# The recurrence of a decoder block: its output products and two blocks' gating on GpSimd, and its side work in a new order

## The chip, the cores and the metric

The kernel runs on one core of a Trainium2 chip. The core has a matmul engine (PE), a vector engine (DVE), an activation engine (ACT), GpSimd (POOL) and a queue for transfers (SP). The metric is the device time of one execution in microseconds (us), lower is better.

## The reference, cut to what matters

A decoder layer over x (2 sequences of 1024 tokens, 256 wide), in three parts, each followed by a residual sum and a layer norm: a gated linear recurrence, an attention over 64 context rows picked by an index list, and a feed-forward part with its own attention and 8 experts. The change lies in the first part and in the preparation of the second.

```
def _L0_attn_ref(x, Wq, Wk, Wv, Wgk1, Wgk2, bgk2, Wg, gnw, Wo):   # 16 heads, DK = 8, DV = 16
    q, k, v = x @ Wq, x @ Wk, x @ Wv
    gk = jax.nn.log_sigmoid(x @ Wgk1 @ Wgk2 + bgk2) / 16.0
    def step(h, inp):
        qt, kt, vt, gt = inp
        h = h * jnp.exp(gt)[..., None] + kt[..., None] * vt[..., None, :]
        ot = jnp.einsum('bhk,bhkv->bhv', qt * scale, h)
        return (h, ot)
    ...
    o = o * jax.lax.rsqrt(jnp.mean(o * o, axis=-1, keepdims=True) + EPS) * gnw
    o = o * (g * jax.nn.sigmoid(g))                               # g = x @ Wg
    return o.reshape(Bx, Tx, VDIM) @ Wo
...
x = _layernorm(x + _L0_attn_ref(...))
x = _layernorm(x + _L0_xattn_ref(x, ctx, indices, ...))   # softmax over 64 picked context rows
x = _layernorm(x + _L0_ffn_ref(x, ...))
```

For the second part the kernel doesn't gather: it counts, per token, how often each of the 64 context rows is in the index list, and adds the logarithm of the count to the scores.

## The kernel before

The program is a few blocks of work with a barrier of all engines between them. The first, `front`, holds the recurrence; `cross_blocks` follows, then the attention and the experts. In each, every engine has its own list of instructions, written out by hand in the order in which it runs them; semaphores tie the lists together. An engine that waits holds up all that is behind it in its list.

The recurrence keeps (head, key index) on the 128 partitions and the 1024 tokens of one sequence along the row. One **step** jj (32 of them, `NJ`: 16 value indices for each of two sequences) does:

- PE, `values(jj)`: four matmuls that spread one value index over the partitions, into PSUM banks 0 and 1 or 2 and 3 (`2 * (jj % 2)`), two steps ahead of their use.
- DVE, `product(jj)` (L521): values times keys, from PSUM into a slot of the ring `qh` (6 slots, `RQ`).
- DVE, `state(jj)` (L526): the scan over the tokens with `decay`, in place in `qh`.
- DVE, `output(jj)` (L531): `qh` times the queries `QT`, in place.
- Each fourth step, with q the number of the four: PE `sums(q)` (L314) adds the 8 key indices of a head for those four steps; ACT `sums_out(q)` copies the sums out, PE `turn(q)` transposes them, ACT `tokens(q)` writes them into `O`, token by token. Banks 4 and 5 carry this, and all the other projections in turn.

DVE's list is `state(jj)`, side work of the step, `product(jj + 1)`, `output(jj)`, more side work. Side work is written as `if jj == ...` in each engine's list: the second sequence's projections and gates, the low parts of values (`parts_lo`) and of x (`x_lo`), output gates (`output_gates` on PE, `silu` on ACT), weights of the second part (`wqo`, `udc`, `ckv`, `kv`), and the counting. For this ACT makes 65 **indicators** (`signs`, L696, tile `c_hot`: the sign of index minus a constant, ring of 6 slots, `RS`), and PE's `counts(u)` sums four at a time into banks 6 and 7. The table `taken` says how many indicators ACT has made by each step, and `count_at` derives from it the step of each `counts(u)`.

When a sequence's outputs are whole, its two blocks of 512 tokens go on: ACT squares (`out_square`), DVE sums per head (`out_means`), ACT takes the root (`out_root`), DVE `out_gated` (a reciprocal L846, `O` times it L848, times the gates L850), PE transposes, ACT copies, PE multiplies with `Wo` and adds x (`out_product`), DVE takes the statistics from PSUM (`out_stats`), ACT writes the normed rows (`out_rows`). Blocks 0 and 1 are done inside the recurrence (steps 17 to 28), 2 and 3 in `cross_blocks`. At step 30 DVE spreads the second part's keys and values (`Kblk`, L602, and `Vblk`). After step 31 come the last indicator, the counts' way out (`cntT`), and the first pieces of the second part; then the barrier.

## Time and profile before

| | us |
|---|---|
| median of 3 runs | 1363.28 (1363.03 to 1363.65) |
| the profiled execution, its own time | 1363.14 |
| its span in the profile | 1361.4 |
| recurrence, from the first scan to the end of the last indicator | 24.58 to 193.98 |
| next block's first matmul | 208.86 |

The profiled execution is within 0.2 us of the median, and 1.7 us of it lie outside the span; all places below are us from the span's start. Busy shares say which engine could be the limit; what ends last at a place is read from the order in time and from the idle time in brackets.

### The profile page before, as it was taken

Reading aid. Unit: us, or ns where it says so; the run is one execution under the profiler, and the core shown is the slowest. Engines: PE = TensorE matmul, PEld = TensorE weight load, DVE = VectorE, ACT = ScalarE, POOL = GpSimd, SP = SyncE. Lnnn points to the kernel's source line nnn. Section 1 sums busy time; section 2 is a strip of 40 time slices with the busy share of each in tenths; the row PEclk is TensorE's granted clock in tenths of the full one; section 3 lists DMA queues with packets and bytes.
Section 4 is the critical chain, followed back from the end, with each engine's and each line's share of the span. In section 5 each row is a group of like instructions: output and inputs, shape, how many; then the busy total and the mean of one; then the engine's idle time right before and its main releaser. Section 6 shows DMA issues by size and latency. Waiting matters only on the chain.

```text
span 1361.4 us, 19541 instructions
## 1 busy us (share of the span) xinstructions
PE 1283.8 (94%) x7802; PEld 953.8 (70%) x7802; DVE 973.9 (72%) x1481; ACT 642.8 (47%) x942; POOL 140.5 (10%) x225
## 2 busy tenths in 40 slices
PE   8787768999899999999999999999999999999997
PEld 6354436677655555558888788888888888888886
DVE  7899997787798998848676655655646556555566
ACT  5687764346468877874332432323323223233233
POOL 5000003000523423310000000000000000000000
PEclk9898889999999999999999999999999999999999
DMA  5000001004602221203000011201101102010001
GB/s 140 1 1 1 0 1 36 2 1 147 209 27 67 64 56 51 68 20 109 17 1 17 16 58 43 70 16 39 47 8 47 39 17 70 16 39 16 0 16 47
DMA packets 40332, 55.82 MB, mean 41 GB/s; under 512 B 9553, under 2 KB 26625, under 8 KB 40241
## 3 DMA queue, kind: packets, MB, share of 16 engines
q1 hardware_dynamic: 35056, 43.67, 10.5%
q0 software_dynamic: 3648, 10.09, 2.6%
q8 instruction: 62, 1.02, 0.3%
q10 hardware_dynamic: 1536, 0.81, 0.2%
q14 instruction: 30, 0.24, 0.1%
HBM read 43.73 MB, written 10.55 MB: 40 GB/s over the span
## 4 chain that ended last, share of the span: by engine, by line
PE 52%; DVE 2%; ACT 0%; issue 0%; ACTq 0%; DVEq 0%
PE PS L2513 25%; PE PS L2526 24%; PE PS L2276 1%; PE PS L114 0%; PE PS L2539 0%; PE PS L2257 0%; PE PS L2290 0%; DVE OT_all L2674 0%; DVE r_st L2352 0%; DVE r_on L2369 0%; DVE r_on L2349 0%; PE PS L2551 0%; DVE X L2361 0%; DVE x_mid L2665 0%; ACT X L2635 0%
## 5 line engine op out<-in xcount | busy, mean ns | idle before, releaser
L2596 ACT ACTIVATE x_g<-PS,x_bias 128x512 f32<-128x512 f32 x256 | 175.9, 687 | 493.4 <-PE PS L2513 493.3
L2513 PE MATMUL PS<-x_h,x_w 128*128 128x512 f32 x1536 | 398.7, 395 | 0.0
L2526 PE MATMUL PS<-x_mid,x_w 128*128 128x512 f32 x1488 | 383.9, 393 | 1.1 <-DVE x_w L2248 1.1
L2513 PEld LDWEIGHTS PS<-x_h,x_w 128*128 128x128 f32 x1536 | 286.1, 188 | 64.7
L2526 PEld LDWEIGHTS PS<-x_mid,x_w 128*128 128x128 f32 x1488 | 279.2, 188 | 65.7 <-DVE x_w L2248 1.6
L2665 DVE CAST x_mid<-x_g 128x512 fp32r<-128x512 f32 x256 | 109.2, 427 | 267.3 <-ACT x_g L2596 266.9
L2115 DVE TENSOR_REDUCE a_M<-PS 128x2 f32<-128x1024 f32 (+1 forms) x144 | 173.1, 1223 | 24.5 <-PE PS L1812 18.2
L2667 DVE TENSOR_TENSOR x_mid<-x_g,x_mid 128x512 fp32r<-128x512 f32 x256 | 177.3, 693 | 8.8
L2053 ACT ACTIVATE f_parts<-PS 128x512 f32<-128x512 f32 x224 | 120.8, 601 | 36.2 <-PE PS L1866 24.8
L1889 PE MATMUL PS<-f_parts,aV 128*32 128x256 f32 (+1 forms) x960 | 75.1, 394 | 0.2 <-POOL f_parts L1700 0.2
L696 ACT ACTIVATE c_hot<-c_idxT,c_cid 128x1024 bf16<-128x1024 bf16 x65 | 70.6, 1138 | 5.2 <-PE PS L337 3.9
L526 DVE TENSOR_TENSOR_SCAN qh<-decay,qh 128x1024 f32<-128x1024 f32 x32 | 73.0, 2281 | 0.0
L2493 POOL DMA_DIRECT2D x_wb<-route_w x31 | 16.9, 545 | 476.1 <-DVE OT_all L2674 450.1
L1866 PE MATMUL PS<-aQ,aK 64*128 64x512 f32 x192 | 50.8, 485 | 0.5 <-ACT f_h L2053 0.5
L1866 PEld LDWEIGHTS PS<-aQ,aK 64*128 64x128 f32 x192 | 20.3, 183 | 37.1 <-ACT f_parts L2053 27.0
L2674 DVE SCALAR_TENSOR_TENSOR OT_all<-PS,x_bias,x_wb 128x512 f32<-128x512 f32 x62 | 46.2, 745 | 0.0
L1700 POOL TENSOR_SCALAR_AFFINE_SELECT f_parts<-f_parts 128x512 f32<-128x512 f32 x45 | 28.7, 637 | 161.9 <-ACT f_parts L2053 142.4
L307 PE MATMUL PS<-vparts,g_sel 128*128 128x512 f32 x128 | 39.5, 433 | 5.5 <-DVE qh L521 4.9
L1808 PE MATMUL PS<-aK,aQ 64*128 64x512 f32 (+3 forms) x256 | 36.2, 327 | 7.2 <-PEq L1061 2.8
L2248 DVE TENSOR_TENSOR x_w<-x_raw,x_w 128x1024 fp32r<-128x1024 f32 x32 | 39.4, 1233 | 1.4 <-ACT x_w L2243 1.4
L521 DVE TENSOR_TENSOR qh<-PS,KT 128x1024 f32<-128x1024 f32 x32 | 38.6, 1205 | 1.2 <-PE PS L314 1.2
L531 DVE TENSOR_TENSOR qh<-qh,QT 128x1024 f32<-128x1024 f32 x32 | 38.9, 1214 | 0.0
(385 smaller groups left out, 1577.9 us busy)
## 6 DMA issues: line engine op xcount, KB each, us to landing
x_raw<-L_ffn_e_w SPq DMA_DIRECT2D x32, 512.0 KB, 3.8
qk_parts<-f_parts SPq DMA_DIRECT2D x16, 512.0 KB, 3.5
x_wb<-route_w POOLq DMA_DIRECT2D x31, 256.0 KB, 3.4
aQ<-qk_parts SPq DMA_DIRECT2D x96, 64.0 KB, 2.5
aK<-qk_parts SPq DMA_DIRECT2D x60, 64.0 KB, 2.7
X<-x SPq DMA_DIRECT2D x4, 512.0 KB, 7.5
aK<-qk_parts SPq DMA_DIRECT2D x36, 48.0 KB, 2.0
out<-X SPq DMA_DIRECT2D x3, 512.0 KB, 3.5
```

The costliest lines, as they stand in the source:

```text
L526: e.tensor_tensor_scan(qh[:, jj % RQ, :], decay[:, batch(jj // HD)], qh[:, jj % RQ, :], 0.0, ALU.mult, ALU.add).then_inc(s_h, 1)
L696: e.activation(hot[:, n % RS, :], self.idxT[:, :], ACT.Sign, bias=self.cid[:, c:c + 1], scale=2.0).then_inc(s_sg, 1)
L1866: last = e.matmul(bank, K[q][R, s, tile(TB * h if kind == "k0" else kind)], Q[q][R, s, q0:q0 + BLK], start=True, stop=True)
L1889: last = e.matmul(PS[32 * j:32 * j + 32, 7, dst:dst + w], Vs[m % 2][:, kt, j, :], x, start=k in (0, 3) and half == 0, stop=k in (2, NQD - ...
L2053: e.activation(buf[k][:, j, :], PS[:, 4 + b % 3, :], ACT.Exp).then_inc(A.sem, 1)
L2115: e.tensor_reduce(dst, src, AX.X, ALU.max, negate=True).then_inc(VC.sem, 1)
L2513: last = e.matmul(PS[:, f % 2, :], w1[n % 2][u][:, kt, f * P:(f + 1) * P], self.rows(v, k)[:, kt, :], start=m == 0 and kt == 0, stop=m == ...
L2526: last = e.matmul(PS[:, 2 + 2 * (it % 2) + d, :], w2[n % 2][v][:, f, d * P:(d + 1) * P], mid[u][:, f % RM, :], start=f == 0 and m == 0, st ...
L2596: e.activation(g[s % RG][:, :], PS[:, f % 2, :], ACT.Gelu, bias=b1[:, n, f:f + 1]).then_inc(A.sem, 1)
L2665: e.tensor_copy(mid[0][:, f % RM, :], g[s % RG][:, :]).then_inc(V.sem, 1)
L2667: e.tensor_tensor(mid[1][:, f % RM, :], g[s % RG][:, :], mid[0][:, f % RM, :].bitcast(F32), ALU.subtract).then_inc(V.sem, 1)
L2674: e.scalar_tensor_tensor(out=(y if n else sumT[k])[:, d, :], in0=PS[:, 2 + 2 * (it % 2) + d, :], scalar=b2[:, n, d:d + 1], in1=wb[:, it % ...
```

## The change

It does the following.

1. `output(jj)` for steps 0 to 30 goes from DVE to GpSimd's list; output 31 stays on DVE. `product(jj)` writes back into the PSUM banks that it read, and `state(jj)` scans from there into `qh`. `values(jj)` now waits for `state(jj - 2)` (s_h) where it waited for `product(jj - 2)` (s_kv). `qh` has 7 slots.
2. Of 65 indicators, 17 go to GpSimd (`indicator`, a comparison), 48 stay on ACT. `counts(u)` waits for both. A comparison gives 0 or 1 where the sign gives -1 or 1, so new constants (`fix`, `winb`) correct the counts.
3. For blocks 0 and 1 GpSimd does the two products of the gating (`out_gated_pool`), and the normed rows (`out_rows_pool`); DVE keeps the reciprocal (L905 of the changed kernel). ACT stores the unnormed rows in X (`out_stored`), and DVE's statistics read them there. `Kblk` is spread by GpSimd too.
4. `sums_out`, `turn` and `tokens` work in halves of 512 tokens. The side work of PE, ACT and DVE stands at other steps.

The diff, cut to its core (of the new order of side work only some lines, of `taken` the new table's line):

```diff
-        RQ, RS = 6, 6
+        RQ, RS = 7, 6
...
-            self.og[m] = z[:, :].rearrange("p (t d) -> p t d", t=TB)
+            self.og[m] = (KT[:, 0:T] if m else z[:, :]).rearrange("p (t d) -> p t d", t=TB)
...
+        of_scalar = [n for n in range(NCTX) if n % 4 < 3]
+        taken = list(itertools.accumulate((2, 2, 1, 0, 0, 2, 2, 1, 0, 0, 1, 2, 2, 1, 3, 1, 2, 1, 2, 1, 0, 1, 2, 2, 3, 1, 2, 3, 2, 1, 3, 2)))
+        count_at = [next((jj for jj in range(5, NJ) if taken[jj - 1] >= 3 * u + 3), NJ) for u in range(16)]
+        def output(e, jj):
+            e.wait_ge(s_h, jj + 1)
+            if jj % HD == 0:
+                e.wait_ge(A.sem, A.at(f"q{jj // HD}"))
+            e.tensor_tensor(qh[:, jj % RQ, :], qh[:, jj % RQ, :], QT[:, batch(jj // HD)], ALU.mult).then_inc(s_qh, 1)
...
+                def indicator(u):
+                    if u:
+                        e.wait_ge(s_cnt, min(u, 15))
+                    n = 4 * u + 3 if u < 16 else NCTX
+                    e.tensor_scalar(hot[:, n % RS, :], self.idxT[:, :], float(3 * 16 + u), None, ALU.is_ge).then_inc(s_hot, 1)
+                def keys(b, g):
+                    e.tensor_tensor(Kblk[:, b, g, :, :], kT[...], self.m16[...], ALU.mult).then_inc(s_kblk, 1)
+                e.wait_ge(A.sem, A.at("idx"))
+                indicator(0)
+                for jj in range(NJ - 1):
+                    output(e, jj)
+                    for u in range(1, 16):
+                        if jj == (5, 6, 8, 12, 14, 16, 18, 20, 23, 24, 26, 27, 28, 29, 30)[u - 1]:
+                            indicator(u)
+                    if jj in (21, 25):
+                        self.out_gated_pool(e, (jj - 21) // 4, s_gate)
+                    if jj in (22, 23, 24, 25):
+                        if jj == 22:
+                            e.wait_ge(A.sem, A.at("kv"))
+                        keys((jj - 22) // KD, (jj - 22) % KD)
+                    elif jj == 28:
+                        self.out_rows_pool(e, 0, s_row)
+                indicator(16)
+                self.out_rows_pool(e, 1, s_row)
...
                     if jj >= 2:
-                        e.wait_ge(s_kv, jj - 1)
+                        e.wait_ge(s_h, jj - 1)
...
-                    e.wait_ge(s_sg, min(4 * u + 4, NCTX + 1))
+                    if u < 16:
+                        e.wait_ge(s_sg, 3 * u + 3)
+                    e.wait_ge(s_hot, u + 1)
...
-                e.wait_ge(s_kv, NJ)
+                e.wait_ge(s_row, 1)
+                e.wait_ge(s_h, NJ - 1)
                 self.c_turn(e, 0)
...
-                    e.tensor_tensor(qh[:, jj % RQ, :], wide(2 * (jj % 2)), KT[:, batch(jj // HD)], ALU.mult).then_inc(s_kv, 1)
+                    e.tensor_tensor(wide(2 * (jj % 2)), wide(2 * (jj % 2)), KT[:, batch(jj // HD)], ALU.mult).then_inc(s_kv, 1)
...
+                    if jj >= RQ:
+                        e.wait_ge(s_s, 2 * ((jj - RQ) // 4) + 2)
+                    e.tensor_tensor_scan(qh[:, jj % RQ, :], decay[:, batch(jj // HD)], wide(2 * (jj % 2)), 0.0, ALU.mult, ALU.add).then_inc(s_h, 1)
...
                 for jj in range(NJ):
                     state(jj)
+                    if jj + 1 < NJ:
+                        product(jj + 1)
+                    else:
+                        output(e, jj)
...
+                    elif jj == 21:
+                        self.out_reciprocal(e, 0)
...
+                    elif jj == 25:
+                        self.out_reciprocal(e, 1)
+                    elif jj == 26:
+                        self.out_stats_stored(e, 0)
...
-                e.activation(self.cntT[:, :], wide(6), ACT.Copy).then_inc(s_fin, 1)
+                e.activation(self.cntT[:, :], wide(6), ACT.Identity, bias=self.fix[:, 0:1], scale=self.fix[:, 1:2]).then_inc(s_fin, 1)
...
+    def out_gated_pool(self, e, m, done):
+        og = self.og[m]
+        e.wait_ge(self.OV[m].sem, self.OV[m].at("rs"))
+        e.tensor_tensor(self.by_head(og), self.by_head(self.out_tiles(self.O, m)), self.o_rs[m][:, :].unsqueeze(2).broadcast_to((P, TB * H, HD)), ALU.mult).then_inc(done, 1)
+        e.wait_ge(done, 2 * m + 1)
+        e.tensor_tensor(og, og, self.out_tiles(self.G, m), ALU.mult).then_inc(done, 1)
...
+    def out_rows_pool(self, e, m, done):
+        e.wait_ge(self.OV[m].sem, self.OV[m].at("nmr"))
+        for t in range(TB):
+            x = self.X[:, m * TB + t, :]
+            last = e.tensor_scalar(x, x, self.o_rstd[m % 2][:, t:t + 1], self.o_nmr[m % 2][:, t:t + 1], ALU.mult, ALU.add)
+        last.then_inc(done, 1)
```

Three places show the order. **DVE, step 19, before** (L526 is the scan, L514 `parts_lo`, L521 the product, L531 the output, L846 to L850 the reciprocal and the gating):

```order
L526 SCALAR_TENSOR_TENSOR qh<-decay,qh 128x1024
L514 TENSOR_TENSOR vparts<-PS,vparts 128x1024
L521 TENSOR_TENSOR qh<-PS,KT 128x1024
L531 TENSOR_TENSOR qh<-qh,QT 128x1024
L846 RECIPROCAL go_rs<-go_rs 128x64
L848 TENSOR_TENSOR z<-O,go_rs 128x1024
L850 TENSOR_TENSOR z<-z,G 128x1024
```

**DVE, step 19, changed** (L574 scan, L567 product, L888 `out_means`, L562 `parts_lo`):

```order
L574 SCALAR_TENSOR_TENSOR qh<-decay,PS 128x1024
L567 TENSOR_TENSOR PS<-PS,KT 128x1024
L888 TENSOR_REDUCE go_ms<-z 128x64
L562 TENSOR_TENSOR vparts<-PS,vparts 128x1024
L574 SCALAR_TENSOR_TENSOR qh<-decay,PS 128x1024
```

Outputs and gating have left the list; between two scans there is one product and the side work, and the scan now follows the product whose result it reads at once.

**GpSimd, end of the first block, before** (L225 and L1062 are the way to the next block):

```order
L943 AFFINE_SELECT c_selaug<-c_selaug 128x256 [waits cs_pool] x4
L250 DMA Wo<-L_attn_Wo 128x2x256
L252 DMA gnw<-L_attn_gnw 16x1 x8
L225 UNCONDITIONAL_BRANCH
L1062 UNCONDITIONAL_BRANCH [waits barrier_Pool_Activation_PE_DVE_SP_gather]
L1064 MEMSET aug 128x4x48
L1065 MEMSET c_halfc 128x128
```

**GpSimd, steps 21 to 24, changed** (L231 output, L910 and L912 gating, L267 keys, L265 indicator; in brackets the semaphores waited for):

```order
L231 TENSOR_TENSOR qh<-qh,QT 128x1024 [waits gs_h]
L910 TENSOR_TENSOR z<-O,go_rs 128x1024 [waits go_dve0]
L912 TENSOR_TENSOR z<-z,G 128x1024 [waits gs_gate]
L231 TENSOR_TENSOR qh<-qh,QT 128x1024 [waits gs_h]
L267 TENSOR_TENSOR c_Kblk<-c_L,c_m 128x512 [waits g_act]
L231 TENSOR_TENSOR qh<-qh,QT 128x1024 [waits gs_h]
L265 TENSOR_SCALAR c_hot<-c_idxT 128x1024 [waits gs_cnt]
L267 TENSOR_TENSOR c_Kblk<-c_L,c_m 128x512
L231 TENSOR_TENSOR qh<-qh,QT 128x1024 [waits gs_h]
L265 TENSOR_SCALAR c_hot<-c_idxT 128x1024 [waits gs_cnt]
L267 TENSOR_TENSOR c_Kblk<-c_L,c_m 128x512
```

A list that was empty there now carries the outputs, the gating behind output 21, the keys and the indicators.

**PE, steps 17 and 18, before** (L307 values, L431 and L434 transposes `udc`, L292 turned values):

```order
L307 MATMUL PS<-vparts,g_sel 128x512 [waits gs_lo,gs_kv]
L307 MATMUL PS<-vparts,g_sel 128x512 x3
L431 MATMUL PS<-ident,c_up 128x128 [waits gs_tok]
L431 MATMUL PS<-ident,c_up 128x128 x3
L434 MATMUL PS<-ident,c_down 128x128 x2
L434 MATMUL PS<-ident,c_ctx 128x128 x2
L307 MATMUL PS<-vparts,g_sel 128x512 [waits gs_lo,gs_kv]
L307 MATMUL PS<-vparts,g_sel 128x512 x3
L292 MATMUL PS<-XTp,Wvp 128x512 [waits g_act]
L292 MATMUL PS<-XTp,Wvp 128x512 x11
```

**PE, steps 20 and 21, changed** (L340 values, L477 and L480 `udc`, L484 `ckv`, L347 `sums`, L354 `turn`):

```order
L340 MATMUL PS<-vparts,g_sel 128x512 [waits gs_lo,gs_h]
L340 MATMUL PS<-vparts,g_sel 128x512 x3
L477 MATMUL PS<-ident,c_up 128x128 [waits g_act]
L477 MATMUL PS<-ident,c_up 128x128 x3
L480 MATMUL PS<-ident,c_down 128x128 x2
L480 MATMUL PS<-ident,c_ctx 128x128 x2
L484 MATMUL PS<-decay 128x128 [waits g_act]
L484 MATMUL PS<-decay 128x128
L340 MATMUL PS<-vparts,g_sel 128x512 [waits gs_lo,gs_h]
L340 MATMUL PS<-vparts,g_sel 128x512 x3
L347 MATMUL PS<-qh,headsum 32x512 [waits gs_qh,g_act]
L347 MATMUL PS<-qh,headsum 32x512 x7
```

The `udc` and `ckv` steps now stand together in step 20, each behind a copy on ACT, ahead of the next values; before, other values and projections stood between them.

## Rows read from the trace of the kernel before

**Rows 1.** Busy time by stretch: span, each engine's busy us (instructions), PE clock, DMA

```profile
24.58:194.00 169.42, 127.03 (x717) 77.92 (x715) 161.62 (x134) 120.38 (x127) 0.00 (x0) 0.89 0.00 1
...
608.00:1361.40 753.40, 741.24 (x3385) 607.08 (x3385) 457.04 (x816) 239.18 (x332) 19.00 (x35) 1.00 0.11 34
```

**Rows 2.** DVE in order of time: first scan, a plain step, gating, last output. Start us, us, instruction

```profile
24.58 2.29 DVE L526 TENSOR_TENSOR_SCAN qh<-decay,qh 128x1024 f32<-128x1024 f32 x1
...
93.50 2.28 DVE L526 TENSOR_TENSOR_SCAN qh<-decay,qh 128x1024 f32<-128x1024 f32 x1
95.70 1.20 DVE L521 TENSOR_TENSOR qh<-PS,KT 128x1024 f32<-128x1024 f32 x1
96.82 1.22 DVE L531 TENSOR_TENSOR qh<-qh,QT 128x1024 f32<-128x1024 f32 x1
97.95 2.28 DVE L526 TENSOR_TENSOR_SCAN qh<-decay,qh 128x1024 f32<-128x1024 f32 x1
...
128.13 0.55 DVE L846 RECIPROCAL go_rs<-go_rs 128x64 f32<-128x64 f32 x1
128.71 1.23 DVE L848 TENSOR_TENSOR z<-O,go_rs 128x1024 f32<-128x1024 f32 x1
129.97 1.23 DVE L850 TENSOR_TENSOR z<-z,G 128x1024 f32<-128x1024 f32 x1
...
195.05 1.23 DVE L531 TENSOR_TENSOR qh<-qh,QT 128x1024 f32<-128x1024 f32 x1
```

**Rows 3.** DVE groups to 270 us: count, busy us, mean ns, idle before

```profile
L526 DVE TENSOR_TENSOR_SCAN qh<-decay,qh 128x1024 f32<-128x1024 f32 x32 | 73.0, 2281 | 0.0
L531 DVE TENSOR_TENSOR qh<-qh,QT 128x1024 f32<-128x1024 f32 x32 | 38.9, 1214 | 0.0
L521 DVE TENSOR_TENSOR qh<-PS,KT 128x1024 f32<-128x1024 f32 x32 | 38.6, 1205 | 1.2 <-PE PS L314 1.2
```

**Rows 4.** GpSimd groups, whole span

```profile
L1700 POOL TENSOR_SCALAR_AFFINE_SELECT f_parts<-f_parts 128x512 f32<-128x512 f32 x45 | 28.7, 637 | 161.9 <-ACT f_parts L2053 142.4 <-ACT f_parts L2073 18.5
...
L1677 POOL TENSOR_TENSOR aV<-V,f_bv 128x512 f32<-128x512 f32 x8 | 10.3, 1284 | 0.8 <-POOLq L1707 0.2
```

**Rows 5.** DVE and GpSimd at work together: at 12 us, and at 352 us

```profile
12.10 1.16 DVE L502 TENSOR_TENSOR Wkp<-c_Kblk,Wkp 128x256 fp32r<-128x256 f32 x1 [0.19 <-ACT Wqp L713]
13.18 0.41 DVE L502 TENSOR_TENSOR Wqp<-c_Kblk,Wqp 128x256 fp32r<-128x256 f32 x1
...
11.82 1.17 POOL L943 TENSOR_SCALAR_AFFINE_SELECT c_selaug<-c_selaug 128x1024 fp32r<-128x1024 f32 x1
...
353.70 1.40 DVE L1516 SCALAR_TENSOR_TENSOR f_parts<-PS,f_bk,f_parts 128x512 fp32r<-128x512 f32 x2
...
352.69 1.30 POOL L1677 TENSOR_TENSOR aV<-V,f_bv 128x512 f32<-128x512 f32 x1
```

**Rows 6.** PE in order of time in the recurrence: start us, us, instruction, idle before

```profile
47.10 3.64 PE L314 MATMUL PS<-qh,headsum 128*32 128x512 f32 x16 [3.25 <-DVE XTp L505]
...
101.34 1.19 PE L307 MATMUL PS<-vparts,g_sel 128*128 128x512 f32 x4
102.36 3.03 PE L283 MATMUL PS<-Wgp,XTp 128*128 128x256 f32 x24
...
109.55 1.93 PE L314 MATMUL PS<-qh,headsum 128*32 128x512 f32 x16 [0.27 <-ACT c_WoutT L768]
...
118.35 0.60 PE L431 MATMUL PS<-ident,c_up 128*128 128x128 f32 x4
```

**Rows 7.** ACT in order of time: `udc` copy, root's table load, `ckv` copy, last indicators

```profile
119.42 0.60 ACT L776 ACTIVATE decay<-PS 128x512 f32<-128x512 f32 x1 [1.12 <-PE PS L434]
...
124.71 1.28 ACT L841 ACT_TABLE_LOAD   x1
...
187.39 0.38 ACT L794 ACTIVATE c_L<-PS 128x256 f32<-128x256 f32 x1
187.65 6.33 ACT L696 ACTIVATE c_hot<-c_idxT,c_cid 128x1024 bf16<-128x1024 bf16 x6
```

389 lines of the change are left out of this document (207 added, 182 removed).

## The prediction, made before the changed kernel ran

> **What bounds the kernel now.** I read the busy time by stretch first. From 608 us on PE works 741.24 of 753.40 us, so nothing but PE's own work counts there, and the change doesn't touch it. The stretch from 24.58 to 194 is the recurrence, 169.42 us, and there DVE works 161.62, PE 127.03, ACT 120.38 and GpSimd nothing [rows 1]. Then I read DVE's instructions in order of time. A plain step starts at 93.50 and the next at 97.95: 4.45 us, as scan to product 2.20, product to output 1.12, output to scan 1.13, with no gap [rows 2]. 32 such steps are 142 us; the rest is side work. The groups say the same: 73.0, 38.6 and 38.9 us, no idle time to speak of before them [rows 3]. DVE's list sets the pace. The last ACT indicators end at 187.65 + 6.33 = 193.98 [rows 7], and the next block's first matmul comes at 208.86, 14.9 us later. In the changed kernel the same chain follows the last indicator: counts, their copy, transposes, DVE's pieces. So the question is where the last indicator ends, and the time moves by as much.
>
> **DVE's list up to step 21.** The output, 1.13 us of each step, leaves. The scan now stands right behind the product that it needs. A pair that depends on each other so is the gating: it starts at 128.71 and at 129.97, 1.26 apart, where independent ones start 1.12 apart [rows 2]. So a step is 2.20 + 1.26 = 3.46 us. That the product writes PSUM and the scan reads it has no row. The nearest: a product that reads PSUM takes 1205 ns, one from the SBUF 1214 [rows 3]. I take no difference; from -0.01 to +0.06 us for each of 64 instructions the bounds are -1 and +4 us. State 21 ends after 21 steps and a scan, 21 x 3.46 + 2.28 = 74.9, plus seven pieces of side work of some 1.13 each (`parts_lo` three times, `x_lo` twice, `log_sigmoid`, `out_means`), 7.9: 82.8 us.
>
> **What PE adds there.** `values(jj + 2)` now waits for `state(jj)`, and its product is due when `state(jj + 1)` ends: from 8 us the room shrinks to under 3.5. PE's list has other pieces between two `values` (1.0 from its start to the next piece's, 101.34 to 102.36 [rows 6]). With two steps' 6.9 us, two `values` and about 1 us of hops, a piece of up to 3.8 us hides. Most do: `output_gates` is 3.0, a sum 1.9 at full rate [rows 6]. Where pieces stand close they don't: steps 13 to 16 have sums with a turn that waits for ACT's copies, then two `output_gates` with a table load between them. By adding them up I find DVE held 1.0 and 1.9 us there, 0.2 at step 9 and 1.2 at step 19, where `parts_lo(3)` waits for ACT's copy of the turned values. Together 4.3 us. PE at half rate is dearer: the sums after an idle time of 3.25 us took 3.64 us, others 1.93 [rows 6]. The clock over the stretch is 0.89 [rows 1]; with shorter gaps I take one such spell on the path, 1.7 us.
>
> **DVE and GpSimd in each other's way.** At 12.10 a DVE subtraction with both inputs in the SBUF took 1.16 us; the next, of the same form, took 0.41. GpSimd's select ran from 11.82 to 12.99: DVE stood until it ended. At 353.70 two DVE instructions with one SBUF input and one from PSUM took 1.40 together, beside a GpSimd product of 1.30 us; that is what others of GpSimd's products take, 1284 ns [rows 4, 5]. So one kind waits and the other doesn't. New products and scans are of the second kind: the scan's other input is in PSUM. Only `log_sigmoid(1)` (z and decay) is of the first; it meets an output in flight, half of 2.46 us, 1.2 us. The Trainium skill's page "SBUF — State Buffer", section "Who interferes with whom", puts it as a rule, two SBUF inputs against a GpSimd instruction that reads the SBUF; the trace agrees, and by it these 1.2 us stand and no others.
>
> State 21 ends at 24.58 + 82.8 + 4.3 + 1.7 + 1.2 = 114.6.
>
> **GpSimd's list.** Its product of 128x512 takes 1284 ns; a select takes 637 for 512 columns and 1.17 us for 1024, so some 107 ns are fixed [rows 4, 5]. An output of 1024 columns is then 2 x 1284 - 107 = 2.46 us (between 2.3 and 2.57). It hides under DVE's 3.46, with the indicators of 1.17 (the select's time; the comparison has no row, 0.9 to 1.5). From step 21 it doesn't: the gating of block 0 starts when DVE's reciprocal is there. Behind that stand nine outputs (22.1), four gating products (9.8), four keys of 1.28 (5.1), eight indicators (9.4) and one block's rows, four of 0.37 (1.5): 47.9 us, where DVE has ten steps and some 7 us of side work, 42. GpSimd sets the end. A block's gating products take DVE 2.4 us now [rows 2] and will take GpSimd 4.9.
>
> **The reciprocal comes late.** PE's step 20 is a chain, counted from the end of state 20: `values` 1.1, `udc` transposes 1.2 (the row at 118.35 is half of it), ACT's two copies 1.1, `ckv` 0.7, its copies 0.7, the root's table load 1.28 and root 0.35, reciprocal 0.55, six hops 0.6 [rows 2, 6, 7]: 7.6 us, 4.1 past the end of state 21. DVE stands in front of the reciprocal for 2.2 of them; GpSimd starts the gating then.
>
> **Waits at the end.** PE's `counts(u)` wait for GpSimd's indicators, PE's product of block 1 for the gating, ACT's copy for PE, and ACT's last six indicators (1.05 each [rows 7]) for all of these. Followed through, `counts(14)` is done 2.7 us after GpSimd could start indicator 15, and ACT's last indicator ends within 0.5 us of GpSimd's. Last indicator: 114.6 + 4.1 + 47.9 + 2.7 = 169.3. Before it was 193.98: 24.7 us less. ACT's saving, 17 indicators of 1.05, is 18 us off the path. The profiled execution, 1363.14, lies 0.14 under the median, 1363.28, and I subtract from the median: 1338.6 us.
>
> **Rivals.** (1) *GpSimd and PE keep up.* Outputs of 2.3 us, indicators near 1.0, no wait of 4.1 or 2.7: 13 products at 0.16 less are 2.1, eight indicators at 0.17 less 1.4, and the waits go but for 2: 8.3 us more, 33 less than now, 1330. For it, the waits are sums of small hops that may overlap; against, lists in order rarely lose nothing. DVE's own list with no wait (82.8, ten steps 34.6, side work 7.0, last output 1.2: 125.6) would end 46 us earlier than now, when the last output ends at 195.05 + 1.23 [rows 2]: 1317, a floor. (2) *PE's order binds.* PE's 127 us at clock 0.89 in 145 us are 88%. If each of the seven turns in the loop holds PE 1.2 us for ACT's copies on the path (8.4), and the 4.3 double: 12.7 back, 12 us less, 1351. (3) *DVE and GpSimd take turns*, the side that ends slower: place, every step; if a scan or product stands for the whole output, a step is 3.46 + 2.46 = 5.9 us where it was 4.45, 31 x 1.45 = 45 us more, 1408. It decides from 1.0 us of each output not covered. For it: the 1.16 us at 12.10; against: the pair at 353.70 [rows 5]. The Trainium skill's "Perfetto Trace Analysis", section "Optimizing Scalar/DVE Operations", warns that moving work between these two may not help, since they share a read port: this rival. (4) The saving is eaten altogether, within 0.2%: needs (2) twice.
>
> **The numbers.** Forecast 0.57, (1) 0.13, (2) 0.20, (3) 0.08, (4) 0.02. A measurement of this kernel can tell about 0.2% from no change, 2.7 us. Faster 0.90, same 0.02, slower 0.08. The range holds (1) and (2) and PSUM's bound: 1325 to 1354.
>
> **What would show it.** DVE steps of 3.46 us and no product over 1.25 or scan over 2.35; `log_sigmoid` longer than 1.22; GpSimd outputs near 2.46, back to back only after step 21; DVE idle before the reciprocal for ACT; the last indicator near 169 us, the time from there to the next block unchanged, near 14. Scans of 3 us or outputs of 4 would show (3); `values` late in most steps, (2). If the next block starts later than the last indicator says, my reading of the tail is wrong.

## The result, and the profile after

| | before | after |
|---|---|---|
| median, us | 1363.47 (4 runs, 1363.03 to 1365.45) | 1351.9 (4 runs, 1350.68 to 1353.2) |
| ratio, 95% interval | | 0.9915, 0.9899 to 0.9931 |
| profiled span, us | 1361.4 | 1349.5 |
| state 21 ends | | 119.76 (forecast 114.6) |
| last indicator ends | 193.98 | 181.80 (forecast 169.3) |
| next block's first matmul | 208.86 | 197.20 |

The change is worth 11.6 us; the forecast was 24.7 (1338.6 us). The time lies in the stated range, 1325 to 1354, but more than half of the forecast gain is missing.

Busy time by stretch of the changed kernel (columns as in [rows 1]):

```profile
24.58:182.00 157.42, 121.97 (x719) 79.44 (x718) 127.34 (x97) 103.58 (x119) 134.46 (x61) 0.92 0.00 1
596.00:1349.50 753.50, 741.26 (x3385) 607.09 (x3385) 456.77 (x816) 239.14 (x332) 18.87 (x35) 1.00 0.11 34
```

The recurrence takes 157.42 us instead of 169.42. DVE's busy share fell from 95% [rows 1] to 81%, and GpSimd works 134.46 us, 85%. After it nothing has changed: from 596 us on PE works 741.26 us, against 741.24 in [rows 1].

DVE in order of time (start us, us, instruction, idle before it and who ended that): a plain step, the waits at 61, 67 and 103 us and the long subtraction ahead of state 21, state 21, the reciprocal, and a wait behind it.

```profile
28.39 2.29 DVE L574 TENSOR_TENSOR_SCAN qh<-decay,PS 128x1024 f32<-128x1024 f32 x1
30.59 1.21 DVE L567 TENSOR_TENSOR PS<-PS,KT 128x1024 f32<-128x1024 f32 x1
31.84 2.29 DVE L574 TENSOR_TENSOR_SCAN qh<-decay,PS 128x1024 f32<-128x1024 f32 x1
...
61.37 1.23 DVE L567 TENSOR_TENSOR PS<-PS,KT 128x1024 f32<-128x1024 f32 x1 [2.52 <-PE PS L340]
...
67.07 1.23 DVE L567 TENSOR_TENSOR PS<-PS,KT 128x1024 f32<-128x1024 f32 x1 [2.15 <-PE PS L340]
...
71.65 2.53 DVE L559 SCALAR_TENSOR_TENSOR z<-z,decay 128x1024 f32<-128x1024 f32 x1
...
103.49 1.23 DVE L567 TENSOR_TENSOR PS<-PS,KT 128x1024 f32<-128x1024 f32 x1 [4.30 <-PE PS L340]
...
117.47 2.29 DVE L574 TENSOR_TENSOR_SCAN qh<-decay,PS 128x1024 f32<-128x1024 f32 x1
...
122.61 0.55 DVE L905 RECIPROCAL go_rs<-go_rs 128x64 f32<-128x64 f32 x1 [1.73 <-ACT go_rs L892]
...
162.38 1.23 DVE L567 TENSOR_TENSOR PS<-PS,KT 128x1024 f32<-128x1024 f32 x1 [3.01 <-PE PS L340]
```

DVE's groups, and GpSimd's (count, busy us, mean ns of one, idle before):

```profile
L574 DVE TENSOR_TENSOR_SCAN qh<-decay,PS 128x1024 f32<-128x1024 f32 x32 | 72.9, 2278 | 1.4 <-PE PS L347 0.8
L567 DVE TENSOR_TENSOR PS<-PS,KT 128x1024 f32<-128x1024 f32 x32 | 38.9, 1214 | 13.8 <-PE PS L340 13.8
...
L231 POOL TENSOR_TENSOR qh<-qh,QT 128x1024 f32<-128x1024 f32 x31 | 73.5, 2376 | 17.2 <-DVE qh L574 17.2
L265 POOL TENSOR_SCALAR c_hot<-c_idxT 128x1024 bf16<-128x1024 bf16 x17 | 47.1, 2769 | 7.0 <-ACT c_idxT L765 4.2 <-PE PS L374 2.5
L953 POOL TENSOR_SCALAR X<-X,go_rstd,go_nmr 128x256 f32<-128x256 f32 x8 | 4.3, 554 | 0.0
L267 POOL TENSOR_TENSOR c_Kblk<-c_L,c_m 128x512 f32<-128x512 f32 x4 | 4.2, 1052 | 0.0
```

The step is what it was to be: 31.84 - 28.39 = 3.45, a scan 2278 ns, a product 1214, although one writes and the other reads PSUM. GpSimd's output takes 2376 ns. Its indicator takes 2769, where 1.17 us had been put.

GpSimd in order of time from state 21 on, then PE (three places ahead of state 21, and the end of the stage) and ACT:

```profile
121.59 2.36 POOL L231 TENSOR_TENSOR qh<-qh,QT 128x1024 f32<-128x1024 f32 x1
123.91 1.93 POOL L910 TENSOR_TENSOR z<-O,go_rs 128x1024 f32<-128x1024 f32 x1
...
176.22 5.60 POOL L265 TENSOR_SCALAR c_hot<-c_idxT 128x1024 bf16<-128x1024 bf16 x2
181.80 2.17 POOL L953 TENSOR_SCALAR X<-X,go_rstd,go_nmr 128x256 f32<-128x256 f32 x4
...
57.96 1.98 PE L306 MATMUL PS<-c_L,Wgk 16*128 16x512 f32 x4 [2.16 <-ACT c_L L784]
...
62.23 3.86 PE L296 MATMUL PS<-XTp,Wkp 128*128 128x512 f32 x12
...
97.90 4.63 PE L316 MATMUL PS<-Wgp,XTp 128*128 128x256 f32 x24 [1.75 <-ACT V L712]
...
179.12 1.05 PE L371 MATMUL PS<-c_hot,c_win 128*32 128x512 bf16 x8 [3.85 <-POOL c_hot L265]
181.87 1.04 PE L374 MATMUL PS<-c_hot,c_win 128*32 128x512 bf16 x2 [1.71 <-POOL c_hot L265]
...
197.20 0.98 PE L1196 MATMUL PS<-XTp,vparts 64*128 64x256 f32 x12 [1.31 <-PEq L233]
...
175.30 2.17 ACT L738 ACTIVATE c_hot<-c_idxT,c_cid 128x1024 bf16<-128x1024 bf16 x2
```

From 123.91 to 181.80 GpSimd runs without a gap: 57.9 us for the list that was put at 47.9. ACT is done with its indicators at 177.47; PE waits 3.85 and 1.71 us for GpSimd's last two, and the next block follows as before, 15.4 us behind the last indicator (14.9 before).

### The profile page after: what moved, and what is told of

Read it like the earlier page. It is cut to its first block, busy times and chain, and to the rows that moved or that the text cites. A ratio compares the mean times of both kernels' runs of the same rounds, so it can differ in the third digit from the quotient of the medians.

```text
span 1349.5 us, 19595 instructions
## 1 busy us (share of the span) xinstructions
PE 1280.6 (95%) x7802; PEld 957.5 (71%) x7802; DVE 936.8 (69%) x1442; ACT 626.0 (46%) x936; POOL 277.6 (21%) x297
## 4 chain that ended last, share of the span: by engine, by line
PE 52%; DVE 2%; ACT 0%; issue 0%; ACTq 0%; DVEq 0%
PE PS L2602 25%; PE PS L2615 25%; PE PS L2365 1%; PE PS L114 0%; PE PS L2628 0%; PE PS L2346 0%; PE PS L2379 0%; DVE OT_all L2763 0%; DVE r_st L2441 0%; DVE r_on L2458 0%; DVE r_on L2438 0%; PE PS L2640 0%; DVE X L2450 0%; DVE x_mid L2754 0%; ACT X L2724 0%
## 5 line engine op out<-in xcount | busy, mean ns | idle before, releaser
L2204 DVE TENSOR_REDUCE a_M<-PS 128x2 f32<-128x1024 f32 (+1 forms) x144 | 173.1, 1223 | 24.2 <-PE PS L1901 18.0
L231 POOL TENSOR_TENSOR qh<-qh,QT 128x1024 f32<-128x1024 f32 x31 | 73.5, 2376 | 17.2 <-DVE qh L574 17.2
L574 DVE TENSOR_TENSOR_SCAN qh<-decay,PS 128x1024 f32<-128x1024 f32 x32 | 72.9, 2278 | 1.4 <-PE PS L347 0.8
L738 ACT ACTIVATE c_hot<-c_idxT,c_cid 128x1024 bf16<-128x1024 bf16 x48 | 52.5, 1136 | 11.4 <-PE PS L371 10.1
L265 POOL TENSOR_SCALAR c_hot<-c_idxT 128x1024 bf16<-128x1024 bf16 x17 | 47.1, 2769 | 7.0 <-ACT c_idxT L765 4.2
L567 DVE TENSOR_TENSOR PS<-PS,KT 128x1024 f32<-128x1024 f32 x32 | 38.9, 1214 | 13.8 <-PE PS L340 13.8
L1955 PEld LDWEIGHTS PS<-aQ,aK 64*128 64x128 f32 x192 | 20.4, 183 | 37.0 <-ACT f_parts L2142 26.0
L340 PE MATMUL PS<-vparts,g_sel 128*128 128x512 f32 x128 | 37.3, 415 | 6.7 <-DVE qh L574 5.8
```

The lines of the kernel that those rows point to most:

```text
L231: e.tensor_tensor(qh[:, jj % RQ, :], qh[:, jj % RQ, :], QT[:, batch(jj // HD)], ALU.mult).then_inc(s_qh, 1)
L574: e.tensor_tensor_scan(qh[:, jj % RQ, :], decay[:, batch(jj // HD)], wide(2 * (jj % 2)), 0.0, ALU.mult, ALU.add).then_inc(s_h, 1)
L738: e.activation(hot[:, n % RS, :], self.idxT[:, :], ACT.Sign, bias=self.cid[:, c:c + 1], scale=2.0).then_inc(s_sg, 1)
L1955: last = e.matmul(bank, K[q][R, s, tile(TB * h if kind == "k0" else kind)], Q[q][R, s, q0:q0 + BLK], start=True, stop=True)
L2204: e.tensor_reduce(dst, src, AX.X, ALU.max, negate=True).then_inc(VC.sem, 1)
```

## The experiments

Each kernel was compared with the kernel before on the same chip; the changed kernel was measured twice, and beside it ran only e6, e7 and e8 (with its second measurement). From one such comparison to the next the median before lay between 1360.6 and 1363.5 us, so the ratios are compared; the column in us is the ratio times 1361 (1363.5 for the first row), less that. "Stage" is the start of the next block's first matmul in the profiled run, "rest" the span from there to the end. Stage and rest come from one profiled execution of each kernel, so small differences in them mean little: e14 and e16 have the same lists up to state 21, and it ended at 122.1 and 120.1 us. The named runs:

| run | edit to the changed kernel | ratio (95%) | us to before | stage | rest |
|---|---|---|---|---|---|
| before | | 1 | 0 | 208.86 | 1152.5 |
| the change | none, first measurement | 0.9915 (0.9899-0.9931) | -11.6 | 197.20 | 1152.3 |
| e5_change | none, second measurement | 0.9937 (0.9919-0.9954) | -8.6 | 197.42 | 1152.2 |
| e2_late_dve | late 8 indicators on DVE | 0.9888 (0.9873-0.9902) | -15.2 | 188.75 | 1155.4 |
| e3_early_dve | early 9 indicators on DVE | 0.9954 (0.9939-0.9968) | -6.3 | 200.11 | 1153.4 |
| e4_gate_dve | gating on DVE | 0.9937 (0.992-0.9954) | -8.6 | 201.01 | 1153.9 |
| e6_gates_later | one gate product later on PE | 0.9929 (0.9909-0.9949) | -9.7 | 193.68 | 1153.3 |
| e7_both | e2 and e6 | 0.9864 (0.9847-0.988) | -18.5 | 186.48 | 1153.1 |
| e8_twice_late | 2 late indicators twice | 0.9979 (0.9967-0.999) | -2.9 | 204.17 | 1155.2 |
| e9_twice_early | 2 early indicators twice | 0.993 (0.9912-0.9948) | -9.5 | 199.03 | 1153.1 |
| e10_fill | fills for the 17 indicators | 0.985 (0.9834-0.9865) | -20.4 | 185.60 | 1153.0 |
| e12_fill_gates | e10 and e6 | 0.9837 (0.982-0.9854) | -22.2 | 183.53 | 1155.7 |
| e13_two_ops | indicator with a second operation | 1.0004 (0.9992-1.0017) | +0.5 | 206.29 | 1154.9 |
| e14_two_ops_gates | e13 and e6 | 1.0007 (0.9995-1.0019) | +1.0 | 208.47 | 1153.7 |
| e16_and_signs | e14, two ACT indicators earlier | 1.0005 (0.9994-1.0015) | +0.7 | 206.40 | 1153.2 |
| e17_dve_signs | e7, two ACT indicators earlier | 0.9875 (0.9858-0.9892) | -17.0 | 187.93 | 1154.0 |
| e18_split | e17, two indicators back on GpSimd | 0.9852 (0.9837-0.9866) | -20.1 | 187.41 | 1152.2 |

The theory after the result: GpSimd's list sets the end from state 21 on, and the indicator in it costs 1.6 us more than had been put. The rival: PE's order and ACT's chains hold the stage in any case.

### What the indicator costs (e1_ops, e11_ops2, e15_ops3)

> The cost by itself: as soon as the indices stand in their tile, GpSimd runs two fills and eight more instructions on 128x1024 elements, each after the one before has ended: the comparison with bf16 in and out, with f32 in and out, f32 in and bf16 out, bf16 in and f32 out; the product with one number in bf16 and in f32; the bf16 comparison on half the columns; a copy in f32. Nothing is left out of the rest. The comparison that the change gives to GpSimd took 2.77 us a piece where I had put 1.17. If it is the comparison that is slow, the two products take 1.2 to 1.5 and the four comparisons 2.8. If it is the 16-bit type, the f32 comparison takes 1.2 to 1.5 (or 2.2, four times the 0.54 of a row product of 128x256) and the bf16 product 2.8. If it is GpSimd's pace for any arithmetic on one input, all lie at 2.1 to 2.8 and the half at 1.4. The whole kernel becomes later by no more than the sum of these instructions, about 20 us.

Three lists of single instructions on GpSimd, ahead of its first indicator, of this form:

```
+ e.memset(F, 1.0).then_inc(s_m, 1)
+ for out, src, op in ((Bf, Bf, ALU.is_ge), (F, F, ALU.is_ge), (Bf, F, ALU.is_ge), (F, Bf, ALU.is_ge), (Bf, Bf, ALU.mult), ...):
+     e.wait_ge(s_m, 2 + nm)
+     e.tensor_scalar(out, src, 1.0, None, op).then_inc(s_m, 1)
```

The first list on GpSimd, in order of time (`Bf` bf16, `F` f32):

```profile
29.57 2.80 POOL L277 TENSOR_SCALAR c_hot<-c_hot 128x1024 bf16<-128x1024 bf16 x1
32.45 2.77 POOL L277 TENSOR_SCALAR c_Kblk<-c_Kblk 128x1024 f32<-128x1024 f32 x1
...
41.01 2.78 POOL L277 TENSOR_SCALAR c_hot<-c_hot 128x1024 bf16<-128x1024 bf16 x1
...
46.72 1.49 POOL L277 TENSOR_SCALAR c_hot<-c_hot 128x512 bf16<-128x512 bf16 x1
48.28 1.04 POOL L280 COPY c_Kblk<-c_Kblk 128x1024 f32<-128x1024 f32 x1
```

Comparison or product, bf16 or f32, in or out: all 2.77 to 2.80 us. Only the fill (0.96, ahead of these), the copy (1.04) and half of the columns (1.49) are cheaper. So it is neither the comparison nor the type, and of the three cases of the expectation the last holds. But one row of the changed kernel speaks against "GpSimd's pace for one input": a row product of 128x256, with two operations, takes 554 ns [groups above], four of them 2.17 us for 1024 columns.

> The cost by itself, once more: the changed kernel with two fills and eight instructions in f32 on GpSimd ahead of its first indicator, to find why four row products of 128x256 (two operations, factors from a tile) take 2.17 us and one comparison of 128x1024 with a plain number takes 2.77. In turn: multiply and add with factors from a tile on 1024 columns; the same with plain numbers; multiply alone with a factor from a tile; multiply and add from a tile on 256 columns; multiply alone by a plain number on 256; the product of two tiles on 1024; the comparison with a factor from a tile on 1024. If a plain number is what is slow, the forms with factors from a tile take 2.1 to 2.2 for 1024 columns and the others 2.8. If one operation is slower than two, multiply alone takes 2.8 in both forms. If it is the length, 256 columns take under 0.6 in both and 1024 take 2.8 in both.

```profile
29.98 1.20 POOL L280 TENSOR_SCALAR c_Kblk<-c_Kblk,eps 128x1024 f32<-128x1024 f32 x1
31.26 1.05 POOL L282 TENSOR_SCALAR c_Kblk<-c_Kblk 128x1024 f32<-128x1024 f32 x1
32.42 2.85 POOL L284 TENSOR_SCALAR c_Kblk<-c_Kblk,eps 128x1024 f32<-128x1024 f32 x1
35.37 0.56 POOL L280 TENSOR_SCALAR c_Kblk<-c_Kblk,eps 128x256 f32<-128x256 f32 x1
36.01 0.85 POOL L286 TENSOR_SCALAR c_Kblk<-c_Kblk 128x256 f32<-128x256 f32 x1
```

In order: multiply and add with factors from a tile 1.20, with plain numbers 1.05; multiply alone 2.85; multiply and add on 256 columns 0.56, multiply alone 0.85; behind them two tensors 2.37, and the comparison with its factor from a tile 2.84. Two operations are cheaper than one: with the factor from a tile 1.20 against 2.85. That asked for the obvious edit, a comparison with a second operation that does nothing.

> The cost by itself, third list on GpSimd: compare and multiply by a number in bf16 and in f32; multiply and add in bf16; compare and add in f32; multiply twice in f32; add alone in f32; compare and multiply in bf16 on half the columns; a copy in bf16. If only the count of operations decides, all with two take 1.05 to 1.2 us on 1024 columns and the one with one takes 2.8. If multiply and add is a fast case of its own, the other pairs take 2.8 or more. If 16-bit tiles are slower in the two-operation form, the bf16 rows stand out.

```profile
29.69 3.66 POOL L280 TENSOR_SCALAR c_hot<-c_hot 128x1024 bf16<-128x1024 bf16 x1
33.44 3.63 POOL L280 TENSOR_SCALAR c_Kblk<-c_Kblk 128x1024 f32<-128x1024 f32 x1
37.15 1.04 POOL L280 TENSOR_SCALAR c_hot<-c_hot 128x1024 bf16<-128x1024 bf16 x1
38.28 4.77 POOL L280 TENSOR_SCALAR c_Kblk<-c_Kblk 128x1024 f32<-128x1024 f32 x2
```

Compare and multiply takes 3.66 (bf16) and 3.63 (f32), multiply and add in bf16 1.04. The row at 38.28 holds two instructions, compare and add, and multiply twice; in a narrower window the first of them is 3.64 us long, which leaves some 1.1 for the second. Behind them adding alone took 2.78. So on GpSimd two arithmetic operations take 1.05 us (1.20 with factors from a tile), one operation (compare, multiply or add) 2.8, and a comparison with a second operation 3.6. The comparison has no cheap form among those tried. The forecast had its price from a select that took 1.17 us for 1024 columns [rows 5], another instruction.

### Does that price set the time (e13_two_ops, e14_two_ops_gates, e16_and_signs)

> The changed kernel with one word more in GpSimd's indicator: compare, and then multiply by 1.0, in the same instruction; the same result, the same places and waits. The second run of single operations showed 128x1024 with two operations at 1.20 and 1.05 us and with one operation at 2.85. If it is the single operation that is slow, whatever the operation is, the indicator falls from 2.77 to 1.05 to 1.2 us, which is the 1.17 that I had put, and this kernel comes to where the one with fills came: 19 to 22 us under the kernel before. If comparisons are slow in either form (the fast rows so far were multiply and add), it stays at 2.8 us and the kernel within 1 us of the changed one.

```
- e.tensor_scalar(hot[:, n % RS, :], self.idxT[:, :], float(3 * 16 + u), None, ALU.is_ge).then_inc(s_hot, 1)
+ e.tensor_scalar(hot[:, n % RS, :], self.idxT[:, :], float(3 * 16 + u), 1.0, ALU.is_ge, ALU.mult).then_inc(s_hot, 1)
```

GpSimd's group of indicators:

```profile
L265 POOL TENSOR_SCALAR c_hot<-c_idxT 128x1024 bf16<-128x1024 bf16 x17 | 61.7, 3628 | 7.0 <-ACT c_idxT L765 4.2 <-PE PS L374 1.0 <-PE PS L371 0.8
```

The cheap price was expected and the dear one came, 3628 ns: neither of the two cases in the expectation. As a measurement it is as good as a dose: 0.86 us more in each of 17 indicators and nothing else, and the whole gain of the change is gone, 1.0004. The stage ends 9.1 us later. State 21 ends where it did, at 119.96; GpSimd's gating behind it starts 1.0 us later, since the indicator just ahead of output 21 is longer, and the list from there to the last indicator takes 66.2 us instead of 57.9: 8.3 us for eight indicators, of which 6.9 are the dose and the rest small gaps between the instructions. Two kernels stood on top of it:

> Two operations in the indicator and the fourth block's gate product in PE's turn 16. With indicators at 1.05 to 1.2 us: the stage ends 2 us before that of the run with two operations alone (the fills with and without this move: first matmul of the next block at 183.5 and 185.6 us) and the time is 20 to 24 us under the kernel before, about what was forecast for the change. If the stage's gain is given back by half clock in the next blocks, as in the profiled runs with the moved product so far, the time is the same as without it.

```
  elif jj == 14:
      e.wait_ge(s_tok, 6)
      output_gates(2, 4)
- elif jj == 15:
+ elif jj == 16:
      e.wait_ge(A.sem, A.at("G2"))
      output_gates(3, 4)
```

> As the kernel with two operations and the moved gate product, and one step more: ACT takes two of its last six indicators ahead of the seventh sums instead of behind them, where it stood idle for 1.6 and 2.0 us. With GpSimd's list out of the way, the end of the stage was ACT's six indicators in a row behind those sums (6.4 us, PE waiting 3.7 and 2.4 us for them). If this is what ends last, up to 2.2 us less than the kernel without this step; if DVE's or GpSimd's last work is right behind, 0 to 1 us less.

```
- taken = ... 3, 2, 1, 3, 2)))
+ taken = ... 3, 2, 2, 2, 2)))
- early = min((0, 2, ... 1, 1, 1, 0, 1, 0)[jj], taken[jj] - taken[jj - 1])
+ early = min((0, 2, ... 1, 1, 1, 2, 1, 0)[jj], taken[jj] - taken[jj - 1])
```

1.0007 and 1.0005: the 20 us were expected of a price that wasn't there. That doesn't say that PE's order is without effect. Here the moved gate product brought state 21 no nearer (122.1 in e14 and 120.1 in e16, against 119.96 in e13); in e14 PE then stood 1.93 us for GpSimd's longer indicator ahead of the sums. In e6_gates_later below, with the shorter indicator, the same move brought it 3.5 us nearer, and the stage followed. What holds in all of them is the distance from the end of state 21 to the stage's end: 77.2 to 77.6 us in the changed kernel, e5, e6 and e9 with indicators of 2.77 us, and 86.3 to 86.4 in e13, e14 and e16 with indicators of 3.63. ACT's two indicators made earlier in e16 changed nothing in that distance (86.30).

### The price taken away (e10_fill, e12_fill_gates)

> What the change would have given at the price that I put on the indicator: the seventeen comparisons on GpSimd are replaced by a fill of the same tile with zeros (0.96 us a piece by the run that measured the operations; my estimate was 1.17), so the counts of a quarter of the contexts come out wrong; every wait, every other instruction and its place stay. Theory (the price of the indicator is the term that failed): GpSimd's list after state 21 falls from 57.9 to 43 us, waits of PE for it go, DVE's end and ACT's last indicators take over at 171 to 174 us, and the kernel is 15 to 19 us under the one before instead of 8 to 12. What is left to the 24.8 us forecast, 6 to 10 us, is then PE's waits ahead of state 21 and ACT's chain at the end. Rival (the price hardly matters, since PE's order holds DVE): within 2 us of the changed kernel.

```
- e.tensor_scalar(hot[:, n % RS, :], self.idxT[:, :], float(3 * 16 + u), None, ALU.is_ge).then_inc(s_hot, 1)
+ e.memset(hot[:, n % RS, :], 0.0).then_inc(s_hot, 1)
```

The fill leaves the comparison out, and the counts of a quarter of the contexts come out wrong; waits and places are the same. The kernel is 20.4 us under the kernel before, where the change is 8.6 and 11.6 under it. GpSimd at the end of the stage, and PE's wait there:

```profile
167.66 1.84 POOL L265 MEMSET c_hot<- 128x1024 bf16 x2 [3.06 <-PE PS L371]
...
166.54 1.04 PE L371 MATMUL PS<-c_hot,c_win 128*32 128x512 bf16 x8 [3.68 <-ACT c_hot L738]
```

GpSimd now waits, 3.06 us, and PE waits for ACT's indicators, 3.68. The end has passed to ACT's chain, as expected; 15 to 19 us had been expected, 20.4 came. The cost of the indicator alone, 1.81 us less in each, is worth 9 to 12 us. All of it lies behind state 21: with nine cheaper indicators ahead of it, state 21 still ended at 119.88.

> The two causes together: the fills in place of the seventeen comparisons (the counts of a quarter of the contexts come out wrong) and the fourth block's gate product in PE's turn 16 instead of 15. If my two terms, the indicator's price and PE's longest wait ahead of state 21, are what separates the forecast of 24.8 us from the result, this kernel lies 18 to 23 us under the one before, 2.5 to 3.7 us under the run with the fills alone in the stage itself. If it lies at the same time as that run, something after state 21 that neither edit touches (ACT's chain to the last indicators) is the end, and state 21 was not.

The edit is that of e10_fill with that of e14_two_ops_gates. 22.2 us under before, and the stage another 2.1 us earlier (183.53 against 185.60), where 2.5 to 3.7 had been expected; by the ratios 0.9837 and 0.985, whose intervals overlap, the step between them is not resolved. With both edits the kernel comes within 2.5 us of the 24.7 forecast. That is in part luck: a fill takes 0.96 us where the forecast had 1.17 (eight of them, 1.7 us), and most of the wait that was taken away stood in the forecast.

### Doses on GpSimd (e8_twice_late, e9_twice_early)

> A dose of GpSimd time after state 21: the indicators of steps 26 and 28 are computed twice, the second time over the first with the same result, 2 x 2.77 = 5.5 us more on GpSimd's list and nothing on another engine. Theory (GpSimd's list is what sets the end from state 21 on): the whole dose arrives, 5 to 6 us more than the changed kernel beside it. Rival (PE's and ACT's chains set it, and GpSimd's indicators hide beside them): 0 to 2 us more.

```
+ twice, s_twice = (11, 13), self.sem("gs_twice")
...
+ if u in twice:
+     e.tensor_scalar(hot[:, n % RS, :], self.idxT[:, :], float(3 * 16 + u), None, ALU.is_ge).then_inc(s_twice, 1)
+     e.wait_ge(s_twice, twice.index(u) + 1)
```

5.5 us more on GpSimd behind state 21 gave 5.6 us more than the changed kernel on the same chip (1358.34 against 1352.78; the interval of this difference is some 3 us to either side). The dose arrived.

> The same dose of GpSimd time as in the run with two late indicators computed twice (which arrived whole: 5.6 us over the changed kernel), now before state 21: the indicators of steps 6 and 14 are computed twice, 5.5 us more on GpSimd. Theory: GpSimd has gaps there (1.6, 3.4, 1.1 us at 70 to 80, 4.3 us at 107) that take it up, and only what PE waits for that one indicator can reach DVE: 0 to 1.5 us more than the changed kernel. Rival (GpSimd's time counts wherever it is spent): 5 us more.

The same with `twice = (2, 5)`. The same dose ahead of state 21 gave 0.993, against 0.9937: no effect that can be resolved; the stage of the profiled run ends 1.6 us later, and by the intervals up to some 2.5 us can't be excluded, the 5.5 can. GpSimd's time costs little or nothing ahead of state 21 and full price behind it. That is the plainest thing shown here, and it names the list that sets the end.

### Who could take the indicators (e2_late_dve, e3_early_dve)

> The eight indicators after step 21 (of the seventeen) are computed by DVE with the same instruction and the same result; the first nine stay on GpSimd. GpSimd's list from state 21 loses 8 x 2.77 = 22.2 us, DVE gets eight instructions of 0.3 to 1.2 us (its bf16 comparison stands in no trace yet), 3 to 9 us. Theory (GpSimd's list sets the end of this stage): GpSimd's list, 57.9 us from the first gating product on, becomes 36 us and no longer binds; the last indicator (181.8 us now) comes at 174 to 178, when DVE's own list ends with the new work in it, and the time is 1344 to 1348. PE's waits for GpSimd of 3.0, 4.1, 1.7 and 3.9 us go. Rival (PE's order and ACT's chains hold the stage in any case): the last indicator stays at 180 to 183 and the time at 1351 to 1353, with DVE waiting as long as before.

```
+ for u in on_vector:                       # in DVE's list, behind product(jj + 1)
+     if jj == {..., 9: 23, 10: 25, 11: 26, 12: 28, 13: 29, 14: 30, 15: 31, 16: 31}[u]:
+         indicator_on(e, u, s_hotv)        # the same instruction, on DVE
```

15.2 us under before, 0.9888: better than the change; the interval overlaps a little with that of the change's first measurement and lies below that of its second. The last indicator ended at 173.1, 1 us ahead of the expected 174 to 178, and the stage 8.5 us earlier than in the changed kernel; the time, 1345.3, is in the expected range. Its own surprise is the price on DVE:

```profile
130.02 0.48 DVE L221 TENSOR_SCALAR c_hot<-c_idxT 128x1024 bf16<-128x1024 bf16 x1
...
138.83 1.82 DVE L221 TENSOR_SCALAR c_hot<-c_idxT 128x1024 bf16<-128x1024 bf16 x1
...
172.30 0.76 DVE L221 TENSOR_SCALAR c_hot<-c_idxT 128x1024 bf16<-128x1024 bf16 x2
...
138.00 2.36 POOL L238 TENSOR_TENSOR qh<-qh,QT 128x1024 f32<-128x1024 f32 x1
```

The same instruction takes 0.48 us where a GpSimd output was just ending, 0.38 a piece at the end when GpSimd had no work, and 1.82 when a GpSimd output (138.00 to 140.36) was in flight: it ended 0.3 us after that. One engine standing until the other's instruction has ended is what the prediction's rows at 12.10 showed, here called the lock: a bf16 comparison with one SBUF input waits too. The Trainium skill's page "SBUF — State Buffer", section "Who interferes with whom", says that DVE's two-port modes, which `tensor_scalar` can enter, are locked out for a whole GpSimd instruction; the trace agrees, 1.6 to 1.8 us against 0.4.

> The mirror of the run before it: the first nine indicators (before state 21) are computed by DVE, the last eight stay on GpSimd. GpSimd loses 9 x 2.77 = 25 us in a stretch in which it stands idle for some 20 of 88 us, DVE gets nine instructions of 0.3 to 1.2 us in the stretch in which its list is followed back to back. Theory: taking work off GpSimd here is worth nothing, DVE's new work moves state 21 from 119.8 to 123 to 128 (less what it hides in DVE's own waits of 2.5, 2.2 and 4.3 us), and with it the end: 1353 to 1360. Rival (GpSimd's load counts everywhere, through the slots of states and through PE's waits for indicators): faster than 1351.9 by some us.

6.3 us under before, 0.9954: 2.3 us (against the 0.9937 run) or 5.3 us (against 0.9915) worse than the change. Nine indicators of some 1.7 us, 15 us, went into DVE's list; state 21 ended at 123.5, 3.7 us later, since DVE's waits for PE took up most of the rest (1.8 us of them are left of 10.9). That GpSimd lost 25 us ahead of state 21 brought nothing to be seen. The theory held in sign and place, though against the second measurement of the change the intervals overlap; for the price on DVE there had been only bounds.

### The gating part undone (e4_gate_dve)

> The one part 'gating of two blocks on GpSimd' undone: DVE computes the two normalizing and the two gating products right behind its reciprocals (four instructions of 1.2 us, 4.9 us), and GpSimd's list loses 1.93 + 2.36 + 1.95 + 2.35 = 8.6 us. Theory: GpSimd's list ends earlier until it meets DVE's last states, which come 4.9 us later: after state 30 (165.9 us now, some 170.8 then) an output and two indicators of 2.4 + 5.6 us are still due, so the last indicator at 179 (181.8 now) and the time 1349, in any case not over 1352. Rival (DVE's and PE's orders set the end): slower by the 4.9 us that DVE gets, 1356 to 1357.

```
- self.out_gated_pool(e, (jj - 21) // 4, s_gate)      # GpSimd, steps 21 and 25
- self.out_reciprocal(e, m)                           # DVE
+ self.out_gated(e, m)                                # DVE: reciprocal, normalize, gate
```

0.9937, no difference to the second measurement of the change, 0.9937, and 3 us worse than its first, 0.9915. The expected gain of 2.9 us didn't come: in the profiled execution the last indicator ended at 185.7, not 179. That execution took 1356.6 us, 5.3 above the median of the seven, so what its trace shows need not hold in full for the faster ones. DVE at the second gating, and GpSimd beside it:

```profile
148.96 3.28 DVE L899 TENSOR_TENSOR KT<-KT,G 128x1024 f32<-128x1024 f32 x1
152.17 2.27 DVE L572 TENSOR_TENSOR_SCAN qh<-decay,PS 128x1024 f32<-128x1024 f32 x1
...
147.81 3.36 POOL L231 TENSOR_TENSOR qh<-qh,QT 128x1024 f32<-128x1024 f32 x1
...
154.53 2.37 POOL L231 TENSOR_TENSOR qh<-qh,QT 128x1024 f32<-128x1024 f32 x1 [1.38 <-DVE qh L572]
```

The second gating product reads two SBUF tiles, and on DVE it met GpSimd's output: 3.28 us for the product and 3.36 for the output, which take 1.23 and 2.36 alone. State 26 then ended at 154.4, later than GpSimd could have begun its output. From there GpSimd's list to the end is 31 us long in both kernels (151.34 to 181.80 with the change, 154.53 to 185.75 here), six indicators and five outputs, 6 us a step where DVE needs 3.5. The expectation had let GpSimd catch up with DVE over these steps; with that list it didn't. So undoing one part moved the work, and the place where the change puts it is neither gain nor loss that these runs resolve.

### PE's longest wait (e6_gates_later, e7_both)

> The changed kernel with one thing moved on PE: the gate product of the fourth block goes from its turn 15 to turn 16, which is empty, so that PE doesn't stand for ACT's first copy of G (1.75 us) and run 24 matmuls at half clock (4.6 us) while DVE waits 4.3 us for the values of state 17. GpSimd's list is as it was. My account of the change: of the 12.4 us by which state 21 ended later than the bare list of 82.8 us allows, this wait is the largest piece; state 21 ends at 116 to 117 instead of 119.8, GpSimd, which stood idle 4.26 us at the same place, follows, and since its list is packed from there on the whole piece reaches the end: 2.5 to 4.3 us less than the changed kernel beside it. Rival (GpSimd's list alone counts and was late on its own account): no difference over 0.5 us. Rival (the wait only moves to the next sums, which then come behind ACT's second gate): 0 to 1.5 us less.

The edit is the one shown for e14_two_ops_gates. The wait of 4.30 us went (0.61 and 0.16 stood in its place), state 21 ended at 116.5 (119.8 with the change), and the stage 3.7 us earlier than in the changed kernel beside it. In the stage this is as expected. The time fell by 1.6 us (0.9929 against 0.9937) where 2.5 to 4.3 had been expected; the intervals tell it neither from no change nor from what was expected. In the profiled runs 1.1 us went back behind the stage: PE's second group of twelve matmuls in the next block and the busy time of the stretch behind (granted clock after POOL's column), the changed kernel first, then this one.

```profile
199.62 0.98 PE L1196 MATMUL PS<-XTp,vparts 64*128 64x256 f32 x12
...
197.50:205.00 7.50, 6.36 (x56) 4.21 (x56) 6.08 (x6) 3.99 (x5) 7.18 (x11) 1.00 0.01 2
```

```profile
195.88 1.65 PE L1196 MATMUL PS<-XTp,vparts 64*128 64x256 f32 x12
...
196.00:203.00 7.00, 7.00 (x41) 5.12 (x42) 5.43 (x6) 1.76 (x3) 6.83 (x7) 0.52 0.00 0
```

The same twelve matmuls take 1.65 us instead of 0.98: PE's granted clock is 0.52 over 7 us where it was 1.00, so nearly all of it lies at the lower level, 1.2 instead of 2.4 GHz. The column "rest" of the table goes from 1152.2 to 1155.7 us for the same instructions, and PE's busy time in it from 1124.4 to 1128.5. That is most of it, not all: in e8 the rest is 3.1 us longer than in e5 and PE's busy time only 1.1.

> The late eight indicators on DVE (as in the run with that edit alone) and the gate product a turn later, both in one kernel. If the two causes add, as two terms of one sum: 15.2 us under the kernel before from the first, and 2.5 to 4.3 more from the second, 1341 to 1343 where before is 1361. If what binds without GpSimd's indicators is a wait on another engine at the end (ACT's last indicators at 173 us), the second brings nothing there: 1345.

0.9864, 18.5 us under before, 1343.3 us: at the edge of the first case. The stage ends 2.3 us ahead of e2's; by the ratios, 0.9864 and 0.9888, the step isn't resolved. PE's last waits there were 3.68 and 2.69 us for ACT's indicators, hence the last two runs.

### What ends last without GpSimd (e17_dve_signs, e18_split)

> A version with nothing left out: the late eight indicators on DVE, the fourth block's gate product in PE's turn 16, and ACT's two indicators ahead of the seventh sums. Without the last step it was 17.3 us under the kernel before (0.9864), its stage ending with ACT's six indicators in a row and PE waiting 3.7 and 2.7 us for them. If ACT's chain ends last there, 1 to 2 us less (0.985); if DVE's list, 60.8 us busy of 68 with the indicators in it, is right behind, no difference.

The edits are those of e7_both and of e16_and_signs. 0.9875: no gain over e7_both, and PE's last wait is now for DVE's indicator. The end passed from ACT to DVE, the second of the two cases.

```profile
172.07 1.05 PE L379 MATMUL PS<-c_hot,c_win 128*32 128x512 bf16 x8 [4.60 <-DVE c_hot L221]
```

> As the kernel beside it, with two of DVE's eight late indicators given back to GpSimd, at the two places where GpSimd stood idle 2.3 and 2.6 us for DVE's states: steps 26 and 29. DVE's list loses 2 x 1.7 us, GpSimd's gains 2 x 2.77. If GpSimd's list no longer binds and DVE's does, 1 to 3 us less than the kernel beside it. If GpSimd's list, with outputs of 2.4 us and an indicator of 2.77 in a step of 3.5, binds again as soon as an indicator stands late in it, 1 to 3 us more: then the indicator belongs on DVE altogether.

```
- on_vector = [9, 10, 11, 12, 13, 14, 15, 16]
+ on_vector = [9, 10, 12, 13, 15, 16]
```

0.9852 (0.9837 to 0.9866), 1340.9 us where before was 1360.6, and 2.8 us under the kernel beside it. The number is that of the expected first case, but the two intervals overlap a little, and in the stage only 0.5 us is to be seen (187.41 against 187.93): PE's last waits, 1.60 and 2.69 us, are for ACT's indicators again. 1.8 us less lie in "rest", 1.5 of them in PE's busy time, and this edit touches no instruction there. Among the kernels that leave nothing out this has the lowest ratio, not resolved from e7_both; its interval lies below both of the change.

## Why the prediction was right or wrong

- **DVE's step**: right. 3.45 us for 3.46; scan 2278, product 1214 ns; the move to PSUM cost nothing.
- **PE holds DVE ahead of state 21**: right in kind, wrong in place and too small. Put were 4.3 us and 1.7 for half clock. Measured are waits of 0.83, 2.52, 2.15, 0.76, 0.29 and 4.30, together 10.9, 4.9 us more. The last three, at steps 15 to 18, are 5.4 us where 2.9 and the 1.7 had been put. The largest has both causes that the text named, two `output_gates` behind each other and ACT's table load between; four ACT indicators (4.23 us from 91.28) stood ahead of that load as well, and the second ran at a granted clock of 0.62 (4.63 us at 97.90; 3.08 for the one before it, at 1.00). The first three, ahead of the products of steps 8 to 10, are 5.5 us where 0.2 had been put: this is what the sum had missed. At 61.37 PE had waited 2.16 us for ACT's low-rank copy in `gate`, and at 67.07 its key projection of 3.86 us (at 62.23) stood between two `values`. The 1.2 put for step 19 came to 0.17, at 112.90. No run takes the waits at steps 8 to 10 away; what e6 and e12 take away is the wait of 4.30.
- **The lock**: right, by 64 scans and products beside GpSimd at their full pace; `log_sigmoid(1)` took 2.53 us (put 1.2 more than 1.2). Of the two rows that the prediction rested on one was weak: GpSimd's product from 352.69 ended at 353.99, 0.3 us into the DVE pair from 353.70 [rows 5]. Two small ones that had been left out, `out_nmr` of 0.64 and 1.62, may be of the same kind.
- **The reciprocal**: right. GpSimd's gating began 4.15 us past state 21 (put 4.1), DVE stood 1.73 (put 2.2).
- **GpSimd's list**: this is the step that failed, by one term, the price of the indicator. Outputs 9 x 2.37 = 21.3 (put 22.1), gating 8.6 (9.8), keys 4.2 (5.1), rows 2.2 (1.5): 0.8, 1.2 and 0.9 less and 0.7 more. The **eight indicators took 22.2 us, put 9.4**: 12.8 more. (The parts add to 58.5, the list is 57.9 long: neighbours overlap a little in the trace.) The sentence was "the select's time; the comparison has no row, 0.9 to 1.5". The range was too narrow for an operation without a row. The fills show what it was worth: with 0.96 in place of 2.77 the kernel came to 20.4 us under before, 9 to 12 us better than the change.
- **Waits at the end, 2.7**: went into GpSimd's list. It was so long that it never had to wait (57.9 us without a gap).
- **The tail**: right, 15.4 us for 14.9.
- **Rivals.** The time, 1351.9, is that of rival (2), 1351, "PE's order binds". Its mechanism had a part in it: PE's waits ahead of state 21 grew by 4.9 us. But behind state 21 GpSimd never stood for PE (57.9 us without a gap), PE's last waits were for GpSimd, and the number came from the indicator's price: that it meets the rival's 1351 is chance. Rival (1) fell with the indicator, although its outputs near 2.3 were nearly right (2.37). Rival (3) fell: no scan or product of the steps stood for GpSimd.
- **The sum.** Last indicator 181.8 against 169.3, 12.5 us: state 21 by 5.2, GpSimd's list and the waits in it by 7.3 (57.9 against 47.9 + 2.7). With 0.5 us more in the tail that is 13.0 of the 13.1 us between the forecast and the result.

What stays open: why one operation is slower than two on GpSimd, what the waits at steps 8 to 10 would give back, and how many us of e6, e7 and e18 are theirs and how many are PE's clock in the blocks behind.

## What to carry to other kernels

Before an operation goes to another engine, look for a row of this very operation with this count of operands and operations there; without one, the bound has to reach to the dearest row of that engine for this size (here the product of two tensors, estimated at 2.46 us, would have been nearer than the select's 1.17, and still short of 2.77: a run of the operation by itself, as e1_ops, is what settles it). Where a list sets the end from some step on, only its work behind that step has a price: the same 5.5 us had no effect that could be resolved ahead of it and cost 5.6 behind it. A cheap instruction that goes to an engine beside a busy one is counted with the wait for the other's instruction: 0.4 us became up to 1.8 on DVE. And a sum that comes near the measured time is checked term by term and place by place: PE's waits were put at the wrong steps.

## What the runs showed of the hardware

- GpSimd, one tensor of 128x1024 and numbers: fill 0.96 us, copy 1.04, multiply and add 1.05 (1.20 with factors from a tile), one operation alone (compare, multiply, add) 2.77 to 2.85, comparison with a second operation 3.63; bf16 and f32 alike. Two tensors: 2.37.
- DVE's bf16 comparison of 128x1024: 0.38 to 0.48 us alone, 1.6 to 1.8 beside a GpSimd output (e2_late_dve), 2.25 at most (e18_split).
- DVE's product and scan with PSUM: 1214 ns for a product that writes PSUM (1205 into the SBUF), 2278 for a scan that reads it (2281 from the SBUF), and neither slower beside GpSimd.
- A DVE product with two SBUF inputs beside a GpSimd product: 3.28 us against 1.23, and GpSimd's 3.36 against 2.36, both in the same 4.4 us (e4_gate_dve).
- The same twelve matmuls behind the stage took 0.98 us at a granted clock of 1.00 and 1.65 near 0.5. Which it is doesn't follow from when the stage ends: 0.98 for ends at 187.41 (e18) and 204.17 us (e8), 1.65 for 185.60 (e10) and 206.29 us (e13).
